# New orders in the attention steps, and the ones product on 256 columns with a sum made by GpSimd

## What is computed

```python
x = x + conv_gate(group_norm(x))            # per-channel gate from mean, max, std
t = to_tokens(x)                             # 8 batches x 256 tokens x 512
t = t + attention(layer_norm(t))             # 16 heads of 32
t = t + ffn(layer_norm(t))                   # shared expert + top 2 of 8 experts
```

```python
scores = softcap * tanh(q @ k.T / sqrt(32) / softcap)
mask = (j <= i) & (i - j < 256)              # causal; all 256 tokens are in the window
probs = softmax(where(mask, scores, -1e30))
attn = probs @ v                             # then @ w_o.T
```

## Time and profile before

| | us |
|---|---|
| median of 3 runs | 743.72 (743.08 to 745.25) |
| the profiled execution | 743.5 |
| its span, first to last instruction | 741.7 |
| first step, one mid step, late, last step with the tail's output projection | 30.55, 38.04, 36.57, 34.14 |

### The profile page before, as it was taken

The page is one execution under the profiler, slowest core; times in us unless marked ns, Lnnn a source line. Parts: engine busy times, 40 slices in busy tenths (PEclk is TensorE's granted clock), DMA queues, the critical chain, the costliest instruction groups (busy, mean ns, idle before and its releaser), DMA issues.

```text
span 741.7 us, 13486 instructions
## 1 busy us (share of the span) xinstructions
PE 651.9 (88%) x4866; PEld 527.1 (71%) x4867; DVE 387.6 (52%) x895; ACT 281.3 (38%) x498; POOL 284.9 (38%) x329
## 2 busy tenths in 40 slices
PE   0214989999999999999899999999799999999992
PEld 0213978878787878788689899999567676676761
DVE  7765354746464656463654996233444444444341
ACT  8641263636364545464624223444221211212210
POOL 1330243333333324241421113865354554545534
PEclk9999999999999999999999999999999999999997
DMA  9700000101010101011206433351855556555443
GB/s 312 313 0 0 1 2 1 58 2 57 0 57 0 57 0 57 0 53 34 86 1 257 128 114 115 114 170 43 297 92 107 99 99 111 93 107 101 97 72 42
DMA packets 24642, 62.07 MB, mean 84 GB/s; under 512 B 3041, under 2 KB 7905, under 8 KB 23073
## 3 DMA queue, kind: packets, MB, share of 16 engines
q1 hardware_dynamic: 14768, 41.16, 15.5%
q0 software_dynamic: 9168, 20.45, 15.0%
q10 hardware_dynamic: 672, 0.03, 0.1%
HBM read 38.56 MB, written 23.07 MB: 83 GB/s over the span
## 4 chain that ended last, share of the span: by engine, by line
PE 79%; DVE 10%; issue 3%; DMA 3%; POOL 2%; ACT 1%; SPq 1%; DVEq 0%; POOLq 0%; ACTq 0%
PE scores L1442 25%; PE PS L1442 22%; PE scores L1770 9%; PE PS L1551 5%; PE scores L1689 5%; PE scores L1537 3%; PE PS L1713 2%; PE PS L1502 2%; DMA wd_sb<-in_wd 1%; DVE rden L1114 1%; DMA T<-in_x 1%; PE PS L1761 1%; PE PS L1491 1%; DVE front L957 1%; DVE front L1061 1%
## 5 line engine op out<-in xcount | busy, mean ns | idle before, releaser
L1442 PE MATMUL scores<-xb,sw_h 128*128 128x256 f32 x512 | 93.9, 284 | 0.0
L617 POOL DMA_INDIRECT out_tokens<-yo,dest x36 | 57.1, 1586 | 83.5 <-DMA out_tokens<-yo,dest 80.5
L1442 PEld LDWEIGHTS scores<-xb,sw_h 128*128 128x128 f32 x512 | 80.6, 191 | 2.1 <-issue 0.4
L1442 PE MATMUL PS<-xt_h,w_h 128*128 128x256 f32 x256 | 76.4, 299 | 3.6 <-issue 2.1
L837 ACT ACTIVATE es<-scores 128x256 f32<-128x256 f32 x39 | 15.0, 384 | 160.4 <-PE scores L1442 160.4
L1770 PE MATMUL scores<-wd_sb,ehT 128*128 x156 | 73.6, 594 | 1.7 <-DVE ehT L1402 1.0
L534 POOL TENSOR_SCALAR_AFFINE_SELECT probs<-probs 128x256 f32<-128x256 f32 x128 | 51.3, 428 | 61.9 <-ACT probs L719 61.7
L1442 PE MATMUL PS<-xt_l,w_h 128*128 128x256 f32 x256 | 73.4, 287 | 0.0
L1442 PE MATMUL PS<-xt_h,w_l 128*128 128x256 f32 x256 | 73.3, 286 | 0.0
L1442 PE MATMUL scores<-xb,sw_l 128*128 128x256 f32 x256 | 72.2, 282 | 0.0
L1114 DVE RECIPROCAL rden<-PS 128x256 f32<-128x256 f32 x32 | 56.1, 1755 | 26.7 <-PE PS L1551 26.7
(11 more groups left out here) (285 smaller groups left out, 1458.0 us busy)
## 6 DMA issues: line engine op xcount, KB each, us to landing
wgu_l<-in_wgu SPq DMA_DIRECT2D x8, 1024.0 KB, 6.7
T<-in_x SPq DMA_DIRECT2D x8, 512.0 KB, 7.8
w_in<-in_wqkvo SPq DMA_DIRECT2D x4, 1024.0 KB, 12.2
x_rows<-x SPq DMA_DIRECT2D x8, 512.0 KB, 2.8
x_cols<-x2T SPq DMA_DIRECT2D x8, 512.0 KB, 2.7
xc<-x_cols SPq DMA_DIRECT2D x8, 512.0 KB, 3.3
out_tokens<-T SPq DMA_DIRECT2D x8, 512.0 KB, 7.5
wd_sb<-in_wd SPq DMA_DIRECT2D x8, 512.0 KB, 7.0
```

Of the source, the lines that this page charges most:

```text
L617: pool.indirect_dma_start(out[:, :], bass.IndirectOffsetOnAxis(dest[:, t:t + 1], 0), yo[:, t % 3, :], None, compute_op=ALU.add).then_inc(y ...
L1442: ins = pe.matmul(out, lhs(k, a), rhs(k, b), start=m == 0, stop=m == len(products) - 1)
```

## The change

- POOL: after the two `affine_select` of a pair, it waits for its own result (semaphore `masked_late`) and adds the two 128-column blocks of the last 128 queries into a new tile `late_sum`, for both heads of the pair in one instruction. `mask_done` is counted after that.
- PE: the ones product is made of four matmuls of 128 columns on `probs` (the first 128 queries) and four of 128 columns on `late_sum`. The product with `v` is as before.
- Steps first, mid and late: PE does K1 ahead of HV3 (before: behind it), and DVE copies K1 out ahead of `normalise(b, 3)`. DVE takes each `bn_stats` apart: the one of tile 0 right behind the addition to tile 0, the one of tile 1 behind `xt_low`.
- Last step, in a function of its own on each engine: PE puts OP0 between scores 1 and 2, OP1 between HV0 and scores 4, HV2 right behind scores 7, X2T and the gate logits among the shared expert's chunks, and the tail's OP0 and OP1 with the logits between them. It waits for V1's copy at HV0 and no longer ahead of scores 0. ACT splits the first tokens (`split_high`) after pair 3 instead of ahead of pair 0. On POOL the masks of pairs 0 to 3 come in a row, then `att_low(0)`, then `rstd`. DVE normalises group 0 between the two additions to `T`.
- Small tiles move in SBUF to make room for `late_sum`.

```diff
@@ gpsimd, mask
-                ins.then_inc(mask_done, 1)
+                ins.then_inc(masked_late, 1)
+                pool.wait_ge(masked_late, 8 * b + p + 1)
+                t = probs[:, p % 4, :].rearrange("p (h q) -> p h q", h=2)
+                pool.tensor_tensor(late_sum[:, p % 4, :, :], t[:, :, P:S], t[:, :, S:S + P],
+                                   ALU.add).then_inc(mask_done, 1)
@@ vector, step
                 if has_back:
+                    added_stats(part, b - 1, b, 1)
                     tile_variance(var2_ready)
...
                 if has_front:
                     project_out(part, "Q1", b)
+                    project_out(part, "K1", b)
                 normalise(b, 3)
...
-                if has_front:
-                    project_out(part, "K1", b)
@@ tensor, head_values
-                for off, lhs in ((0, lambda h, tt: v[:, tt, h * D:(h + 1) * D]), (S, lambda h, tt: ones[:, 0:D])):
...
+                for tt in range(TT):
+                    for j in range(HC):
+                        h = HC * c + j
+                        early = probs[:, (h // 2) % 4, 384 * (h % 2):384 * (h % 2) + P]
+                        ins = pe.matmul(od_bank[j * D:(j + 1) * D, S + tt * P:S + (tt + 1) * P], ones[:, 0:D],
+                                        late_sum[:, (h // 2) % 4, h % 2, :] if tt else early, start=True, stop=True,
+                                        skip_group_check=True)
@@ tensor, step
                 if has_front:
                     heads_projection(part, "Q1", b)
...
+                if has_front:
+                    heads_projection(part, "K1", b)
                 head_values(b, 3, first)
                 if has_front:
-                    heads_projection(part, "K1", b)
                     values_projection(part, b, 0)
@@ tensor, the new last step
+            def last_step(b):
+
+                for p in (0, 1):
+                    head_scores(b, p, False)
+                pe.wait_ge(att_l_done, 4 * b)
+                out_tile("last", b - 1, b, 0)
+                head_scores(b, 2, False)
+                head_scores(b, 3, False)
+                pe.wait_ge(*emptied("late", "V1", b - 1))
+                head_values(b, 0, False)
+                out_tile("last", b - 1, b, 1)
+                head_scores(b, 4, False)
+                head_scores(b, 5, False)
+                head_values(b, 1, False)
+                head_scores(b, 6, False)
+                head_scores(b, 7, False)
+                head_values(b, 2, False)
+                pe.wait_ge(tanh_done, 8 * b + 7)
+                pe.wait_ge(xb_l_done, 1)
+                hidden_chunk(0, 0, True, 0)
...
@@ gpsimd, the new last step
+            def last_step(b):
+                for p in range(4):
+                    mask(b, p)
+                att_low(b, 0)
+                rstd_of(var2_ready, rstd2_ready, b - 1)
+                mask(b, 4)
+                mask(b, 5)
```

More of the change, by code:

```diff
@@ L579, in _ @@
             step(B - 2, False)
[L580 removed]
+            last_step(B - 1)
             def weight_low(m):
@@ L762, in step @@
                     act.wait_ge(x2T_stored, 16 * b)
+            def last_step(b):
+                for p in range(4):
+                    soft(b, p)
+                split_high(0, 0)
+                act.wait_ge(*filled("last", "OP1", b))
+                att_high(b, 0)
+                soft(b, 4)
+                soft(b, 5)
+                att_high(b, 1)
+                soft(b, 6)
+                soft(b, 7)
+                att_high(b, 2)
+                x2_transposed("last", b)
+                att_high(b, 3)
+                act.wait_ge(x2T_stored, 16 * b)
             def split_high(b, parity):
```

121 lines of the change are left out of this document (73 added, 48 removed).

## The result

| | us |
|---|---|
| before, median of 4 runs beside the changed kernel's | 744.06 (743.08 to 745.25) |
| changed kernel, median of 4 runs | 737.69 (737.31 to 739.07) |
| ratio, with its 95% interval | 0.9921 (0.9903 to 0.9939) |
| the profiled execution of the changed kernel, and its span | 737.31, 735.6 |

The change makes the kernel 0.8% faster: 6.4 us of the 8.4 that I had forecast, inside the range of 732 to 739.5. The two spans, 741.7 and 735.6, are 6.1 us apart, and the table says where these lie. The last column is what the prediction had for the same stretch. The late and last step go to the end of the tail's output projection in both kernels.

What follows compares the result with a forecast made beforehand. PE's queue was taken to bound the kernel (79% of the chain of waits). From 743.5: mid steps -8.0, late -0.3, first 0, last -0.1 give 735.1, so 735.3 us as median; 80% range 732 to 739.5.

Steps and rivals of the forecast that it cites:

- The ones product: PE, each of 32 HVs: four matmuls of 256 columns become four of 128, saving 0.22 us each, 7.0 us in all.
- Rival B: Ones product on PE: 128-column matmuls bring nothing behind each other, so it stays as long; 740.8 us, chance 0.05.
- The two waits that go: PE, mid steps: the 1.22 us wait ahead of HV3 and the 0.37 ahead of Q0 disappear through the new orders.
- HV1, the step that was under-sized: Mid step, XN to HV1: PE waits 0.7 to 1.15 us for POOL's additions; HV1 starts 0.05 to 0.5 later.
- Rival A: POOL's additions cost 1.2 to 1.3 us each and HV1 waits some 0.8 longer in six steps; 741 us, chance 0.08.
- First step: HV0 starts near 97.2, not 95.58, behind POOL's additions; net 0 taken, +1.8 us if the clock returns one stretch later.
- Last step: New waits at HV0, scores 7 and HV2 of 5.2 us against savings and old waits; sum -0.1 us (-1.2 to +1.8).
- Late step: Same HV1 wait as a mid step, three shorter ones products (-0.66), no HV3 wait to remove; -0.3 us.
- Rival C: HV1's wait behind scores drops the clock, 1.7 us a fall; 747.3 us, chance 0.04 every step, 0.05 three or four.
- the forecast's case: Whole kernel: the forecast's own terms hold, 732.9 to 738.9 us by their ends; chance 0.70.
- an addition of 0.56 us: POOL's 256-column addition by the Trainium skill's figure: HV1's stall would be 0.35 us, the forecast some 2 us lower.

## Why the prediction was right, and where it was not

**The ones product: right.** It has 0.55 us from its first start to the next work (278.77 to 279.32) where it had 0.76: 0.21, and 0.22 was taken. The kernel with the additions off the path, 0.86 a mid step below the one with all orders and no sum, has the same four times over (0.21). Rival B is out.

**The two waits that go: right.** HV3 and Q0 start without idle time. That K1 is what covers HV3 is shown by the kernel with the sum and K1 alone.

**HV1, the step that was under-sized.** The stretch from XN to HV1 grew by 0.48, at the top of the 0.05 to 0.5 of the working, and 0.28 was taken; this is 1.0 of the 1.05 us that the five mid steps miss. The term that was off is the masks: 1.48 for two pairs, and they took 0.76 and 1.14. `rstd` ended 4.5 us behind XN, as worked out. I had put VectorE's `x` beside the second addition; it stands behind `att` in VectorE's queue, began 5.83 us behind XN, and met the second pair's masks (6.04 to 7.18) in place of the addition. By my own times, with the first pair's masks and addition done at 6.1 and `x` at 6.05 in the rows of before, I could have seen that. The additions themselves were at the lower end, 0.83 and 0.80 with the engine's wait on itself. Rival A (1.2 to 1.3 us each) is out with a mean of 0.77 over all 64. Group of the changed kernel by line (count, busy us, mean ns):

```profile
L545 POOL TENSOR_TENSOR late_sum<-probs 128x256 f32<-128x256 f32 x64 | 49.0, 765 | 5.3
```

**First step.** HV0 was to start 4.5 us behind its scores, and did, at 4.46. The step is 0.7 longer and I had 0, inside the 0 to +1.8 that I gave. My step "PE loses less to the low clock (it stands through half of that stretch)" failed: the fall did not stay where it was. Before, the clock fell as HV0 began (95.8); here it falls about 1 us behind the start of HV0 (96.39) and comes back at about 101. PE lost as much to it as before, and of the +1.61 of waiting only the ones products gave some back (PE is busy 0.91 less, and four of them are 0.84).

**Last step.** The single waits were near: 1.35, 0.38 and 3.60 against 1.4, 0.9 and 2.9, together 5.3 against 5.2. HV2 waits longer because the masks of pair 5 took 1.14 beside `x` and its addition 1.57 beside VectorE's `xb`, an operation with two SBUF inputs. What was wrong is the other side: I had set these 5.2 against 4.1 of old waits, and noted that the windows gave 3.2. By 3.2 the sum is 5.2 - 3.2 - 0.9 = +1.1; measured, without the 0.73 that moved, it is +1.20. Even by 4.1 the terms give +0.2, and not the -0.1 that stands there. The busy times of two windows were the right base and not starts counted.

**Late step.** -0.14 (that is -0.87 less the 0.73 that moved) against -0.3, with HV1's wait of 0.95.

**Rival C** needed the clock to fall behind HV1's wait. It did not, in any mid step of the changed kernel, at 1.03 us in both of its profiles. The kernel with the sum alone shows that this rival was not idle: ahead of HV3, behind 1.95 us, it fell in two of five mid steps, and at the ends it was low for 6.7 and 13.5 us.

**The sum and the range.** The terms that missed all missed to the same side: 1.05 in the mid steps, 0.7 in the first, 0.2 in the late and 1.3 in the last one. The stretch ahead of the first step, which happened to be 0.80 shorter, hides a part of it in the total. The ends that I gave for the forecast's case, 732.9 to 738.9, do not come out of its terms: all lower ends give 732.7 and all upper ones 740.4. And an addition of 0.56 us would, by my own stall of 0.35 against 0.93, have made the five mid steps 2.9 us shorter and not some 2; the additions took 0.72 to 0.74 where nothing stood beside them.

**What I did not ask.** The working set the sum's costs and the orders' gains into one number. Taken apart, the orders are worth 12.6 us (731.73 against 744.29) and the sum, at its place ahead of the product with `v`, costs 6.0; in both, some 3 us are the low clock of the first and the last step, which the profile with all orders and no sum does not have. The rows for it were there: the wait at HV1 (0.7 to 1.15, six times) and the openly lying additions in the first and last steps come to more than the 7.0 us of the ones products. That the cost is mostly the place and not the work is shown by the kernel with the additions off the path, 8.4 us faster than the changed one with the same sums.

## What to carry to other kernels

Where a helper engine prepares an operand for a part of a group of matmuls, let only that part wait: here the counter was moved, and PE waited for a sum that only the last four of sixteen matmuls read. Price each half of a mixed change by itself, since a good order can carry a costly edit. Where a wait of PE is near those behind which the clock fell, count the fall with the wait. And when an engine gets more work, look at what the engine that shares its access to SBUF does at that moment, on both sides.

## What the runs showed of the chip

- POOL and VectorE slow each other by more than the small mark in the earlier trace rows. Beside each other: masks of a pair 1.14 against 0.76; an addition of 128x256 1.57 against 0.73; one of 128x512 2.12 against 1.29; VectorE's two `x` 1.99 against 0.99; its four `front` 1.98 against 1.47 (beside masks in their last part; 1.38 in the first step of the kernel before, with POOL idle). The Trainium skill (SBUF — State Buffer, SBUF: two separate sides) calls the shared pair of ports an exclusive lock, held for a whole instruction. `x` fits that: its second instruction started 0.12 behind the addition of 1.33, took 1.49 where the first took 0.58, and ended 0.28 behind it. That is one instruction of the fifth mid step; no run was made to test the lock.
- The reciprocal of 128x256 reads from PSUM and took 1.74 to 1.76 everywhere, beside POOL's work or not.
- One fall of the clock cost 1.5 to 1.6 us of a step in which nothing else changed (29.01 and 30.59 with the same kernel; 38.83 and 40.36 in the sum alone). It came behind waits of 1.9 us in some executions, with 3.5 in every one, in the last step of the kernel before behind 0.88, and not behind 1.03 or 1.22 in the mid steps. Most falls lasted some 3.4 us; in kernels with the sum there were some of 6.7 and 13.5, which began within the wait.
- Why the old last step beside the sum has runs up to 743.0 is not shown; a fall of 13.6 us, as in the profile of the sum with K1, would explain it.
